# Cross-attention keys and queries transposed by VectorE in 32x32 blocks, scores on eight TensorE tiles

## The chip, the cores and the metric

The kernel runs on one core of one Trainium2 chip. A core has TensorE (matrix products and its weight loads, PE and PEld in the profile), VectorE (DVE), ScalarE (ACT), GpSimd (POOL) and SyncE (SP, which issues the DMAs). The metric is the device time of the whole program in microseconds. Before the change the median of 3 runs is 1757.12 us (1754.75 to 1758.47).

## The reference

One decoder block on x of 32 sequences of 64 tokens, 512 wide: self-attention, cross-attention on a context of the same size, and a feed-forward part, each added to x.

```python
q = (hidden_states @ Wq.T).reshape(bsz, q_len, H, HD).transpose(0, 2, 1, 3)      # H = 32 heads, HD = 128
k = (cross_attention_states @ Wk.T).reshape(bsz, kv_len, KVH, HD).transpose(0, 2, 1, 3)   # KVH = 8
v = (cross_attention_states @ Wv.T).reshape(bsz, kv_len, KVH, HD).transpose(0, 2, 1, 3)
q = _rmsnorm(q, q_norm_w)
k = _rmsnorm(jnp.repeat(k, GROUPS, axis=1), k_norm_w)       # GROUPS = 4 query heads per key head
scores = jnp.einsum('bhqd,bhkd->bhqk', q, k) * scale
probs = jax.nn.softmax(scores + attention_mask, axis=-1)
out = jnp.einsum('bhqk,bhkd->bhqd', probs, v)               # then @ Wo.T
```

The change lies between the normed q and k and the masked scores of this cross-attention.

## The kernel before

The tokens are worked in two halves of 1024, 8 tiles of 128 tokens each (a tile is two sequences). A half goes through self-attention, then cross-attention, then the feed-forward part. Cross-attention runs over the 8 key heads (groups); in each group over 4 chunks of two token tiles. That makes 32 chunks per half. The first three are prepared in `self_attention`, seven turns of a loop (`Fori`) with 4 slots each follow (`cross_attention`), and the last group is written out in `last_turn_and_ffn`, interleaved with the feed-forward part's first steps.

Every engine has its own list of instructions, written out by hand in `slot` and its neighbours; no scheduler changes it. Engines wait for each other by semaphores alone. Slot k of TensorE is a software pipeline over four chunks: `scores2` of chunk k+1, `transpose_probs` of chunk k, `transpose_chunk` of chunk k+2, `values2` of chunk k, `project_chunk_kv` and `project_chunk_q` of chunk k+3, and `outputs` of chunk k (the output projection of its two tiles). Projections are three fp32r products each (L397 to L399, high and low parts); scores, values and transposes are fp32.

- `transpose_chunk` (L646 to L655) transposes the two key tiles (L649, into a bank of acc), the four heads of the queries of one tile (L654, into y) and of the other (L415, into acc). ScalarE takes them out in `transposed_chunk` (L1040, L1043, L1047) into kt and q2t; the product of the two norm weights is applied at L1040, one number per partition.
- `scores2` contracts all 128 of the head's width: a product of 64 queries by 64 keys on 128 rows, two heads on the two column tiles (L670), all 16 into the one bank sc.
- VectorE adds the mask (L1212, `add_and_max`), takes the row maximum (L1218), later the sums (L1223), and scales keys (L1317) and queries (L1320) by their norm factors in `scale_chunk`. GpSimd computes these factors (L1617), subtracts the maximum (L1626) and normalises (L1632). ScalarE takes the exponential (L852) and the transposed probabilities (L856).
- The values' result ot goes out in a high part (ScalarE, L1053) and a low part (VectorE, `outputs_lo`, shown as w_lo<-ot at L1176), which the output projection waits for.
- PSUM has eight banks: two of acc, sc, pt (transposed probabilities), two of ot, two of y.
- Weights come as pieces through three staging buffers, high part by ScalarE (L844), low part by GpSimd (L1613), or by VectorE for two pieces at the end of slot 0.

## Time and profile before

| what | value |
|---|---|
| median of 3 runs | 1757.12 us |
| profiled execution, its own time | 1758.76 us |
| span from its first to its last instruction | 1757.0 us |
| TensorE busy | 1681.7 us, 96% |
| VectorE busy | 940.7 us, 54% |
| ScalarE busy | 742.2 us, 42% |
| GpSimd busy | 656.5 us, 37% |
| share of the chain that ended last | PE 84%, DVE 8%, POOL 3%, ACT 2%, issue 2% |

Busy is the time in which an engine runs an instruction of the program. The chain is followed back from the last instruction, at each step to what released it. Matmuls are pipelined: the time from one start to the next is what counts, and one instruction lasts longer than that.

### The profile page before, as it was taken

To read this page: it belongs to the slowest core of one execution; us is meant where nothing else is said; L and a number is where in the kernel's file an instruction comes from. 1 tells how busy PE (TensorE), PEld (TensorE's weight loads), DVE (VectorE), ACT (ScalarE), POOL (GpSimd) and SP (SyncE) were. 2 spreads that over 40 slices of the span, in tenths; PEclk is the share of its full clock that TensorE was granted. 3 is DMA by queue.
4 is the path that set the end of the run, shared out by engine and by line. 5 is a ranking of instruction groups with operands and counts; after the bars stand their busy time and mean duration, and the time that the engine had idled before them with its cause. 6 is when DMAs were issued, how large, how long until landed. Compare 5 with 4: busy or idle time off the path is not lost.

```text
span 1757.0 us, 29641 instructions
## 1 busy us (share of the span) xinstructions
PE 1681.7 (96%) x11352; PEld 1382.2 (79%) x11352; DVE 940.7 (54%) x1657; ACT 742.2 (42%) x1332; POOL 656.5 (37%) x511
## 2 busy tenths in 40 slices
PE   5999899999999999989988999999999999999898
PEld 5556788888888888778875567888888888887797
DVE  4488454454544454664545874554454545447543
ACT  2575445354444443421225744444443444434221
POOL 3595323233232332550125944232332332326400
PEclk9999999999999999999999999999999999999999
DMA  4110011011010110211121101010120201202000
GB/s 168 55 43 1 7 55 60 0 60 39 20 60 0 60 57 9 72 49 37 50 65 55 31 1 43 19 60 0 60 60 0 60 19 41 66 0 85 6 19 24
DMA packets 25871, 70.92 MB, mean 40 GB/s; under 512 B 3152, under 2 KB 3152, under 8 KB 25808
## 3 DMA queue, kind: packets, MB, share of 16 engines
q1 hardware_dynamic: 25808, 70.05, 12.8%
q8 instruction: 43, 0.70, 0.2%
q14 instruction: 20, 0.16, 0.0%
HBM read 65.85 MB, written 4.19 MB: 40 GB/s over the span
## 4 chain that ended last, share of the span: by engine, by line
PE 84%; DVE 8%; POOL 3%; ACT 2%; issue 2%; DMA 1%; POOLq 0%; SPq 0%; DVEq 0%; ACTq 0%
PE acc L397 14%; PE acc L398 13%; PE acc L399 13%; PE y L397 9%; PE y L398 9%; PE y L399 9%; PE ot L684 4%; PE sc L670 3%; PE pt L438 3%; PE acc L415 2%; PE sc L578 2%; PE y L654 1%; DVE w_lo L1176 1%; DVE pmax L1218 1%; POOL prob L1626 1%
## 5 line engine op out<-in xcount | busy, mean ns | idle before, releaser
L1626 POOL TENSOR_TENSOR prob<-prob,pmax 128x512 f32<-128x512 f32 x128 | 134.0, 1047 | 309.0 <-DVE pmax L1218 308.5
L1304 DVE TENSOR_REDUCE qkss<-kbd 128x4 f32<-128x512 f32 x128 | 87.8, 686 | 291.0 <-ACT kbd L876 291.0
L1617 POOL TENSOR_TENSOR qkrs<-qkve,mhalf 128x10 f32<-128x10 f32 x64 | 125.1, 1954 | 303.4 <-DVE qkve L1310 303.4
L397 PE MATMUL y<-w_hi 128*128 128x512 f32 x576 | 232.5, 404 | 0.9 <-DVE w_lo L1176 0.9
L397 PE MATMUL acc<-w_hi,xn_hi 128*128 128x512 f32 (+1 forms) x576 | 221.0, 384 | 11.2 <-DVE xn_lo L1176 11.2
L398 PE MATMUL y<-w_lo,w_hi 128*128 128x512 f32 x576 | 225.8, 392 | 0.0
L399 PE MATMUL y<-w_hi,w_lo 128*128 128x512 f32 x576 | 225.6, 392 | 0.0
L398 PE MATMUL acc<-w_lo,xn_hi 128*128 128x512 f32 (+1 forms) x576 | 220.2, 382 | 0.0
L399 PE MATMUL acc<-w_hi,xn_lo 128*128 128x512 f32 (+1 forms) x576 | 219.2, 381 | 0.0
L1613 POOL TENSOR_TENSOR w_lo<-stage,w_hi 128x1024 fp32r<-128x1024 f32 (+1 forms) x88 | 170.3, 1953 | 99.4 <-ACT w_hi L844 99.4
L1632 POOL TENSOR_TENSOR prob<-prob,prec 128x512 f32<-128x512 f32 x128 | 148.5, 1160 | 130.7 <-DVE prec L1226 130.7
L856 ACT COPY probt<-pt 128x512 f32<-128x512 f32 x128 | 74.2, 580 | 286.0 <-PE pt L438 286.0
L397 PE MATMUL acc<-w_hi,cx_hi 128*128 128x256 f32 x512 | 150.9, 295 | 1.7 <-DVE xn_lo L1176 1.7
L1176 DVE TENSOR_TENSOR w_lo<-ot,w_hi 128x1024 fp32r<-128x1024 f32 (+1 forms) x80 | 89.3, 1116 | 112.7 <-ACT w_hi L1053 112.4
L875 ACT COPY qb<-acc 128x512 f32<-128x512 f32 x128 | 75.1, 587 | 168.5 <-PE acc L399 168.5
L398 PE MATMUL acc<-w_lo,cx_hi 128*128 128x256 f32 x512 | 144.4, 282 | 0.0
L399 PE MATMUL acc<-w_hi,cx_lo 128*128 128x256 f32 x512 | 144.2, 282 | 0.0
L844 ACT CAST w_hi<-stage 128x1024 fp32r<-128x1024 f32 (+1 forms) x116 | 104.3, 917 | 89.3 <-DMA stage<-in_w_cross 76.7
L397 PEld LDWEIGHTS acc<-w_hi,xn_hi 128*128 128x128 f32 x576 | 110.8, 192 | 30.9 <-DVE xn_lo L1176 7.9
L397 PEld LDWEIGHTS y<-w_hi 128*128 128x128 f32 x576 | 109.0, 189 | 31.8 <-issue 11.4
L399 PEld LDWEIGHTS y<-w_hi,w_lo 128*128 128x128 f32 x576 | 109.1, 189 | 23.2
L399 PEld LDWEIGHTS acc<-w_hi,xn_lo 128*128 128x128 f32 x576 | 110.6, 192 | 20.5
(132 smaller groups left out, 3670.7 us busy)
## 6 DMA issues: line engine op xcount, KB each, us to landing
stage<-in_w_cross SPq DMA_DIRECT2D x64, 512.0 KB, 3.7
stage<-in_w_cross SPq DMA_DIRECT2D x32, 256.0 KB, 2.8
stage<-in_w_ffn SPq DMA_DIRECT2D x16, 512.0 KB, 3.5
x<-in_x SPq DMA_DIRECT2D x8, 512.0 KB, 3.7
stage<-in_w_self SPq DMA_DIRECT2D x8, 512.0 KB, 4.5
kt<-in_ctx SPq DMA_DIRECT2D x16, 256.0 KB, 2.9
out_x<-x SPq DMA_DIRECT2D x16, 256.0 KB, 2.0
stage<-in_w_self SPq DMA_DIRECT2D x4, 256.0 KB, 3.4
```

What stands on the lines that cost most here:

```text
L397: nc.tensor.matmul(target, l_hi, r_hi, start=first, stop=False)
L398: nc.tensor.matmul(target, l_hi, r_lo, start=False, stop=False)
L399: return nc.tensor.matmul(target, l_lo, r_hi, start=False, stop=last)
L844: nc.scalar.copy(target, stage[:, place.slot(n), 0:width]).then_inc(w_hi_done, 1)
L856: nc.scalar.copy(probt[:, buffer, :], pt[:]).then_inc(pt_done.sem, 1)
L875: nc.scalar.copy(qraw[:, 2 * (k % 2) + t], blocks(acc[n % 2]))
L1176: return nc.vector.tensor_tensor(target, whole, high.bitcast(F32), ALU.subtract)
L1304: nc.vector.tensor_reduce(qkss[:, k % 2, t * REP:(t + 1) * REP], qsq[:, t], AX_X, ALU.add).then_inc(q_sum.sem, 1)
L1613: nc.gpsimd.tensor_tensor(low, stage[:, place.slot(n), 0:width], high.bitcast(F32), ALU.subtract).then_inc(w_lo_done, 1)
L1617: return nc.gpsimd.tensor_tensor(target, source, mhalf[:, 0:width], ALU.pow)
L1626: nc.gpsimd.tensor_tensor(pr, pr, spread(pmax[:, buffer, :], 8, SEQ), ALU.subtract).then_inc(s_sub.sem, 1)
L1632: nc.gpsimd.tensor_tensor(pr, pr, spread(prec[:, buffer, :], 8, SEQ), ALU.mult).then_inc(s_nrm.sem, 1)
```

## The change

Keys and queries are no longer transposed by TensorE. VectorE transposes them in 32x32 blocks (`transposed`): a block stays on its 32 partitions, so that partitions 32i to 32i+31 hold block i of 32 tokens with the head's width in four pieces of 32 (j) side by side. A product then contracts 32 rows, and four of them (j = 0 to 3) are added up in PSUM. The 32 queries of block i meet the 64 keys of their sequence, its own 32 and those of the sibling block; ScalarE copies the sibling's keys to the partitions of block i (`sibling_keys`, four copies). The scores of block i go to bank i, since the four row tiles write at the same time; sc, pt and the two banks of ot become one tile, quad, of four banks. The two column tiles hold two pairs of heads. The mask is laid out anew and added in two pieces (`masked_scores`). The norm weights now lie along the free side (wrow) and are applied in `scale_chunk`, two instructions for the keys. The transposed probabilities use y[0] in place of pt. On TensorE the values move behind the projection of keys and values; ScalarE and VectorE have their lists reordered, and ScalarE and GpSimd take output weights 4 first in slot 0.

```diff
@@ TensorE
-            def transpose_chunk(place, k):
...
-                for t in range(2):
-                    ins = nc.tensor.transpose(to[:, t * P:(t + 1) * P], kv[:, 2 * (k % CHUNKS) + t, 0:P], ident[:])
...
-                for h in range(REP):
-                    ins = nc.tensor.transpose(y[0][:, h * P:(h + 1) * P], qraw[:, 2 * (k % 2), h], ident[:])
...
-                transpose_tile(*use(place, k, C_QT), qraw[:, 2 * (k % 2) + 1].rearrange("p h d -> p (h d)"))
             def scores2(place, k):
                 at = place.at
                 pe.wait_ge(qt_done.sem, at(qt_done, k + 1))
-                evacuated(pe, *use(place, k, C_QT))
+                pe.wait_ge(sib_done.sem, at(sib_done, k + 1))
                 pe.wait_ge(s_add.sem, at(s_add, k))
+                pe.wait_ge(ot_lo_done.sem, at(ot_lo_done, max(k - 1, 0)))
                 for t in range(2):
-                    for j in range(2):
-                        for b in range(2):
...
+                    for j in range(4):
+                        for i in range(4):
+                            rows = slice(32 * i, 32 * (i + 1))
+                            first = 32 * (1 - i % 2)
                             for h in range(2):
+                                ins = nc.tensor.matmul(
+                                    quad[h * SEQ:(h + 1) * SEQ, i, t * SEQ:(t + 1) * SEQ],
+                                    q2t[rows, t, j, 2 * h:2 * h + 2, :].rearrange("p h q -> p (h q)"),
+                                    k2t[rows, t, j, first:first + SEQ], start=j == 0, stop=j == 3)
@@ slot
                 scores2(place, k + 1)
-                transpose_probs(place.at, k, k % PRING)
-                transpose_chunk(place, k + 2)
-                values2(place, k)
+                transpose_probs2(place.at, k)
                 project_chunk_kv(place, k + 3)
+                values2(place, k, k + 2)
                 project_chunk_q(place, k + 3)
@@ ScalarE
-                transposed_chunk(place, k + 2)
...
+            def sibling_keys(at, k):
+                act.wait_ge(kt_done.sem, at(kt_done, k + 1))
+                for i in range(4):
+                    o = i ^ 1
+                    first = 64 * (1 - i % 2)
+                    ins = nc.scalar.copy(k2t[32 * i:32 * (i + 1), :, :, first:first + 32],
+                                         k2t[32 * o:32 * (o + 1), :, :, 32:64])
+                ins.then_inc(sib_done.sem, 1)
@@ VectorE
+            def masked_scores(at, k):
+                dve.wait_ge(sc_rdy.sem, at(sc_rdy, k + 1))
+                for t in range(2):
...
+                ins.then_inc(s_add.sem, 1)
+            def transposed(place, k):
+                at = place.at
+                dve.wait_ge(qk_nrm.sem, at(qk_nrm, k + 1))
+                dve.wait_ge(sc_rdy.sem, at(sc_rdy, k))
+                c = k % CHUNKS
+                nc.vector.transpose(k2t[:, :, :, 32:64],
+                                    kv[:, 2 * c:2 * c + 2, 0:P].rearrange("p t (j d) -> p t j d", j=4)
+                                    ).then_inc(kt_done.sem, 1)
+                for t in range(2):
+                    ins = nc.vector.transpose(q2t[:, t],
+                                              qraw[:, 2 * (k % 2) + t].rearrange("p h (j d) -> p j h d", j=4))
+                ins.then_inc(qt_done.sem, 1)
@@ slot
-                add_and_max(at, k + 1, (k + 1) % PRING)
-                outputs_lo(at, k)
+                masked_scores(at, k + 1)
+                row_max(at, k + 1, (k + 1) % PRING)
+                transposed(place, k + 2)
                 sums(at, k + 1, (k + 1) % PRING)
                 key_squares(place, k + 3)
+                outputs_lo(at, k)
```

TensorE's list at the head of the loop, before; qb holds the queries, kt the keys, a row ends with the semaphores that it waits for:

```order
L670 MATMUL sc<-kt,qb 64x64 [waits s_add]
L670 MATMUL sc<-kt,qb 64x64 x15
L436 REGISTER_ALU [waits s_nrm]
L438 MATMUL pt<-ident,prob 128x128 [waits pt_done]
L438 MATMUL pt<-ident,prob 128x128 x3
...
L649 MATMUL acc<-ident,kv 128x128 [waits acc_free1]
...
L654 MATMUL y<-ident,qb 128x128 [waits y_free]
...
L415 MATMUL acc<-ident,qb 128x128 [waits acc_free0]
...
L684 MATMUL ot<-probt,kv 128x256 [waits ot_lo_done]
```

and after, with the lines of the changed kernel:

```order
L656 REGISTER_ALU [waits sib_done,qt_done]
L658 REGISTER_ALU [waits s_add]
L667 MATMUL quad<-kt,qb 64x64 [waits ot_lo_done]
L667 MATMUL quad<-kt,qb 64x64 x63
L677 ISA [waits s_nrm]
L679 MATMUL y<-ident,prob 128x128 [waits y_free]
L679 MATMUL y<-ident,prob 128x128 x3
...
L407 MATMUL acc<-w_hi,cx_hi 128x256 [waits acc_free1]
...
L695 MATMUL quad<-probt,kv 128x256 [waits ot_lo_done,s_add]
```

Ten transposes are gone, the scores are 64 products in place of 16, and the values stand behind the 24 products that project keys and values.

VectorE's list in the last turn, behind the loop, before:

```order
L1212 TENSOR_TENSOR prob<-sc,mask 128x512
L1218 TENSOR_REDUCE pmax<-prob 128x8
L1235 TENSOR_TENSOR x<-y,x 128x512
L1196 TENSOR_SCALAR xn<-x,mv,rstd 128x512
L1176 TENSOR_TENSOR w_lo<-ot,w_hi 128x2x8x64
```

and after:

```order
L1222 TENSOR_TENSOR prob<-quad,mask 128x256 x2
L1243 TENSOR_REDUCE pmax<-prob 128x8
L1233 STREAM_TRANSPOSE kt<-kv 128x8x32
L1237 STREAM_TRANSPOSE qb<-qb 128x512 x2
L1260 TENSOR_TENSOR x<-y,x 128x512
L1204 TENSOR_SCALAR xn<-x,mv,rstd 128x512
L1184 TENSOR_TENSOR w_lo<-quad,w_hi 128x2x8x64
```

The three transposes of chunk 3 of the group stand ahead of the first layer norm of the feed-forward part.

## Rows read from the trace of the kernel before

**Rows 1.** The page: busy shares, and the last chain by engine.

```profile
PE 1681.7 (96%) x11352; PEld 1382.2 (79%) x11352; DVE 940.7 (54%) x1657; ACT 742.2 (42%) x1332; POOL 656.5 (37%) x511
...
PE 84%; DVE 8%; POOL 3%; ACT 2%; issue 2%; DMA 1%; POOLq 0%; SPq 0%; DVEq 0%; ACTq 0%
```

**Rows 2.** A stretch of the loop: length; busy us of PE, PEld, DVE, ACT, POOL; clock.

```profile
400.00:500.00 100.00, 100.00 (x728) 84.49 (x727) 49.53 (x77) 42.98 (x75) 31.56 (x22) 1.00 0.09 26
```

**Rows 3.** The last chain in order of time: start us, length us.

```profile
456.79 1.08 PE sc L670 x32
...
474.58 1.08 PE sc L670 x32
```

**Rows 4.** Timeline of TensorE in one slot: start us, length us.

```profile
474.51 1.15 PE L670 MATMUL sc<-kt,qb 128*64 128x64 f32 x32
475.59 0.66 PE L438 MATMUL pt<-ident,prob 128*128 128x128 f32 x4
476.08 0.38 PE L649 MATMUL acc<-ident,kv 128*128 128x128 f32 x2
476.30 0.60 PE L654 MATMUL y<-ident,qb 128*128 128x128 f32 x4
...
477.27 1.13 PE L684 MATMUL ot<-probt,kv 64*128 64x256 f32 x8
478.33 0.39 PE L397 MATMUL acc<-w_hi,cx_hi 128*128 128x256 f32 x1
...
481.30 0.40 PE L397 MATMUL acc<-w_hi,xn_hi 128*128 128x512 f32 x1
...
486.76 0.39 PE L397 MATMUL y<-w_hi 128*128 128x512 f32 x1
```

**Rows 5.** Products under way in 134.92 to 134.96 and in 477.26 to 477.31.

```profile
L593 PE MATMUL ot<-probt,vbd x4: 297/297/297, 134.9 to 134.9; 128*32 128x128 f32 x4
```

```profile
L684 PE MATMUL ot<-probt,kv x2: 480/480/480, 477.3 to 477.3; 64*128 64x256 f32 x2
```

**Rows 6.** VectorE: one slot's sum, groups of one slot, and the mask of slot 1.

```profile
474.40:492.20 17.80, 17.80 (x127) 15.01 (x126) 8.23 (x14) 6.51 (x12) 4.05 (x3) 1.00 0.00 0
```

```profile
L1176 DVE TENSOR_TENSOR w_lo<-ot,w_hi 128x1024 fp32r<-128x1024 f32 x1 | 1.2, 1224 | 2.5 <-ACT w_hi L1053 2.5
...
L1317 DVE TENSOR_TENSOR kv<-kv,qkrs 128x256 f32<-128x256 f32 x1 | 0.4, 426 | 0.7 <-POOL qkrs L1617 0.7
```

```profile
443.25 0.68 DVE L1212 TENSOR_TENSOR prob<-sc,mask 128x512 f32<-128x512 f32 x1
```

**Rows 7.** ScalarE: groups of one slot, and a small copy.

```profile
L1053 ACT CAST w_hi<-ot 128x1024 fp32r<-128x1024 f32 x1 | 1.0, 1017 | 0.3 <-PE ot L684 0.3
...
L1047 ACT COPY qb<-acc 128x512 f32<-128x512 f32 x1 | 0.6, 609 | 0.0
...
L1040 ACT ACTIVATE kt<-acc,qkn 128x256 f32<-128x256 f32 x1 | 0.5, 481 | 0.0
```

```profile
L972 ACT COPY vbd<-kv x64: 230/242/245, 60.1 to 1019.8; 64x64 f32<-64x64 f32 x64
```

**Rows 8.** The loop's entry: TensorE's timeline.

```profile
207.63 0.43 PE L649 MATMUL acc<-ident,kv 128*128 128x128 f32 x2 [3.78 <-DVE qb L1320]
...
211.44 0.47 PE L397 MATMUL acc<-w_hi,cx_hi 128*128 128x256 f32 x1
```

**Rows 9.** The last turn: TensorE's wait, VectorE and GpSimd at 722.

```profile
729.88 0.66 PE L415 MATMUL acc<-ident,xn 128*128 128x128 f32 x4 [2.27 <-DVE xn L1196]
```

```profile
722.27 2.40 POOL L1613 TENSOR_TENSOR w_lo<-stage,w_hi 128x1024 fp32r<-128x1024 f32 x1
...
722.34 2.62 DVE L1317 TENSOR_TENSOR kv<-kv,qkrs 128x256 f32<-128x256 f32 x1 [0.74 <-POOL qkrs L1617]
```

**Rows 10.** The page: instruction loads, and a load's time to landing.

```profile
q8 instruction: 43, 0.70, 0.2%
...
stage<-in_w_cross SPq DMA_DIRECT2D x64, 512.0 KB, 3.7
```

More of the change, by code:

```diff
@@ L221, in decoder_block @@
         qk_ve, qk_rs, qk_nrm = (count(n, 0, 0, CHUNKS, 0) for n in ("qk_ve", "qk_rs", "qk_nrm"))
-        qt_rdy, qt_done = (count(n, 0, 0, CHUNKS, 0) for n in ("qt_rdy", "qt_done"))
+        kt_done, sib_done, qt_done = (count(n, 0, 0, CHUNKS, 0) for n in ("kt_done", "sib_done", "qt_done"))
         kbd_done = count("kbd_done", 0, NSEQ, 0, 0)
@@ L306, in load_constants @@
             def load_constants():
-                sp.dma_start(qkn[:, 0:1], qn_in).then_inc(const_ld.sem, 16)
-                sp.dma_start(qkn[:, 1:2], kn_in).then_inc(const_ld.sem, 16)
-                sp.dma_start(mask[0:SEQ, :], mask_in).then_inc(const_ld.sem, 16)
-                sp.dma_start(mask[SEQ:P, :], mask_in).then_inc(const_ld.sem, 16)
+                sp.dma_start(qrow, qn_in.rearrange("d o -> o d").to_broadcast([P, HD2])).then_inc(const_ld.sem, 16)
+                sp.dma_start(wrow[:], kn_in.rearrange("d o -> o d").to_broadcast([P, HD2])
+                             ).then_inc(const_ld.sem, 16)
+                for h in range(REP):
+                    for l in range(2):
+                        sp.dma_start(mask[32 * h:32 * (h + 1), l, :], mask_in[32 * l:32 * (l + 1), :]
+                                     ).then_inc(const_ld.sem, 16)
                 sp.dma_start(f1g_raw, f1g_in).then_inc(const_ld.sem, 16)
@@ L635, in self_attention @@
                 project_chunk_q(first, 1)
-                transpose_chunk(first, 0)
                 project_out(at, NT - 1, NT)
@@ L683, in values2, with outputs @@
                         rows = slice(b * SEQ, (b + 1) * SEQ)
+                        probs = probt[rows, k % 2, t * 256:(t + 1) * 256].rearrange("p (l h q) -> p h l q", l=2, h=REP)
                         ins = nc.tensor.matmul(ot[:, b, t * 256:(t + 1) * 256],
-                                               kv[rows, 2 * (k % CHUNKS) + t, P:2 * P],
-                                               probt[rows, k % 2, t * 256:(t + 1) * 256], start=True, stop=True)
+                                               kv[rows, 2 * (k % CHUNKS) + t, P:2 * P], probs, start=True, stop=True)
                 ins.then_inc(ot_rdy.sem, 1)
-            def outputs(place, k, t, queries):
+            def outputs(place, k, t):
                 if t == 0 and k % CHUNKS == 0:
                     pieces_split(place, 5)
-                if t == 0:
-                    pe.wait_ge(qt_done.sem, place.at(qt_done, queries))
                 project_out(place.at, 2 * k + t, k + 1)
@@ L855, in evacuate_probs @@
                 act.wait_ge(pt_rdy.sem, at(pt_rdy, u + 1))
[L856 removed]
+                nc.scalar.copy(probt[:, buffer, :], pt).then_inc(pt_done.sem, 1)
             def output_hi(i):
@@ L874, in queries @@
                 act.wait_ge(q_sum.sem, place.at(q_sum, 2 * k + t - 1))
+                if k >= 2:
+                    act.wait_ge(qt_done.sem, place.at(qt_done, k - 1))
                 nc.scalar.copy(qraw[:, 2 * (k % 2) + t], blocks(acc[n % 2]))
@@ L1126, in last_turn_and_ffn @@
                 split_piece(place, 5)
-                evacuate_probs(turn.at, 3, 1)
+                evacuate_probs2(turn.at, 3)
                 rectify(0, 0)
@@ L1315, in scale_chunk @@
                 c = k % CHUNKS
-                keys = kv[:, 2 * c:2 * c + 2, 0:P]
-                nc.vector.tensor_tensor(keys, keys, spread(qkrs[:, k % 2, 2 * REP:], 2, HD2), ALU.mult)
+                for t in range(2):
+                    keys = kv[:, 2 * c + t, 0:P]
+                    nc.vector.scalar_tensor_tensor(keys, keys, qkrs[:, k % 2, 2 * REP + t:2 * REP + t + 1], wrow[:],
+                                                   ALU.mult, ALU.mult)
                 t = 2 * (k % 2)
@@ L1386, in self_attention @@
                 scale_chunk(first.at, 0)
+                transposed(first, 0)
                 key_squares(first, 1)
@@ L1390, in self_attention @@
                 variance(first.at, 1)
+                updated(7)
                 scale_chunk(first.at, 1)
-                updated(7)
                 key_squares(first, 2)
-                add_and_max(first.at, 0, 0)
+                masked_scores(first.at, 0)
+                transposed(first, 1)
+                row_max(first.at, 0, 0)
                 second_norm(7)
+                query_squares(first, 2, 0)
                 sums(first.at, 0, 0)
-                query_squares(first, 2, 0)
                 query_squares(first, 2, 1)
@@ L1501, in result @@
                                                    ALU.mult, ALU.add).then_inc(x_out.sem, 1)
-                add_and_max(turn.at, 1, 1)
-                outputs_lo(turn.at, 0)
+                masked_scores(turn.at, 1)
+                row_max(turn.at, 1, 1)
+                transposed(turn, 2)
                 sums(turn.at, 1, 1)
                 key_squares(turn, 3)
+                outputs_lo(turn.at, 0)
                 query_squares(turn, 3, 0)
@@ L1512, in last_turn_and_ffn @@
                 final_statistics(0)
-                add_and_max(turn.at, 2, 2)
+                masked_scores(turn.at, 2)
+                row_max(turn.at, 2, 2)
+                transposed(turn, 3)
                 updated(1)
@@ L1524, in last_turn_and_ffn @@
                 norm(2)
-                add_and_max(turn.at, 3, 3)
+                masked_scores(turn.at, 3)
+                row_max(turn.at, 3, 3)
                 norm_lo(1)
```

152 lines of the change are left out of this document (69 added, 83 removed).

## The prediction, made before the changed kernel ran

> **What bounds the kernel now.** I read the busy shares first, then the chain that ended last, then the chain in order of time, and last single slots of the timeline. TensorE is busy for 96% of the span and holds 84% of the last chain; no other engine is over 54% [rows 1]. The reader is to see in the busy times of a stretch that in 400 to 500 us TensorE is busy for every one of the 100 us at clock 1.00, while VectorE has half of its time free [rows 2]. The chain in order of time then shows the loop as a clock: scores (L670) come at 456.79 and again at 474.58, 17.79 us apart, and so slot after slot through both loops [rows 3]. Inside a loop slot nothing but TensorE's own list sets the time. Only at two places per half is it otherwise: at the loop's entry, where TensorE sits idle for 3.78 us [rows 8], and in the last turn, where VectorE is waited for [rows 9]. The kernel has 2 halves of 32 chunks: 28 loop slots, and 4 chunks in the last turn.
>
> One slot of TensorE [rows 4]: scores from 474.51, transposed probabilities from 475.59, transposed keys from 476.08, transposed queries from 476.30, values from 477.27, keys and values projected from 478.33, queries from 481.30, the output projection from 486.76.
>
> **TensorE's part.** The change takes the ten transposes of a chunk away (2 for keys, 8 for queries). They fill 476.08 to 477.27 [rows 4], 1.19 us for ten and the change of tile shape before the values. The four transposes of the probabilities take 0.49, so some 0.11 each after the first; ten cost 1.09 and 0.1 stays as the change of shape, which the new order has as well, between the projection of keys and values and the values. So **-1.09 us per chunk**.
>
> The scores grow from 16 to 64 products in the program, and each runs as two in the trace: 32 now (x32), 128 then. The 32 take 1.08 us: two column tiles run side by side, so that is 16 steps of 64 columns, 67 ns each with the fill. The new ones have the same 64 columns each, on 8 tiles (four of rows by two of columns): 128 / 8 is again 16 steps. What decides is whether eight tiles really overlap. The trace shows it for four and for two: of the values in self-attention four products on four column tiles begin inside a stretch of 40 ns, each 297 ns long, and the two row tiles of the values in cross-attention begin inside 50 ns [rows 5]. So the bound from below is 1.08 (no loss; a gain is excluded, since the steps are as many and as wide). The bound from above is the mean of today's 32 products, 34 ns each: 128 x 34 = 4.3 us. I take the value near the lower one, 1.12: the tiles begin well under 10 ns apart (four in 40 ns, less than their first lasts), and six more of them at some 7 ns lengthen the fill by 0.04. **+0.04 per chunk.**
>
> The Trainium skill (TensorE: Matmul & The Clock Gate, Part 3) has matmuls on different tiles start about 4 ns apart; by that the added fill is 0.02 and the sum would be 1 us better. The same page (Part 1) has start to start never below some 25 ns however small the matmul. If that held between tiles too, 128 x 25 = 3.2 us would stand in place of 1.08, and the kernel would be slower by some 65 us. Rows 5 speak against it: four begin in 40 ns. It is a case of the first rival below, between its ends.
>
> Then 17.79 becomes 17.79 - 1.09 + 0.04 = 16.74 us per slot. The slot that holds chunk 2 of a half I count with the entry, so 27 slots per half: 54 x 1.05 = **-56.7 us**.
>
> **Does another engine hold a slot of 16.7 us?** VectorE gets a transpose of the keys (128x256) and two of the queries (128x512 each), the mask in two pieces, the key scale in two. No row shows a 32x32 transpose. The nearest are two-operand or reducing operations of the same size: 0.43 for 128x256 (L1317), 0.68 for 128x512 (L1212) [rows 6]. I take 0.4 + 2 x 0.7 = 1.8; four times as slow would be 7.2. The mask adds 0.15, the keys 0.15. VectorE's 8.2 us of a slot [rows 6] become 10.3 of 16.7. The wait that could reach TensorE: the output projection needs w_lo of ot (L1176, outputs_lo), and the values now stand behind the projection of keys and values, so only the queries' 5.46 us cover it. Counted from the slot's start, the new order gives: scores to 1.1, probabilities to 1.6, keys and values to 4.5, values to 5.6, queries to 11.1. VectorE: mask 1.3 to 2.2, maximum to 2.9, transposes to 4.7, sums to about 5.6, and L1176 of 1.22 as soon as ScalarE's 1.02 (L1053) is done: 5.9 + 1.0, then to 8.2. It is due at 11.1, so 2.9 us of cover. Transposes up to 4.7 us long cost nothing in a common slot; beyond that the rest shows. ScalarE loses 0.48 + 0.61 + 0.6 = 1.7 us (L1040, L1047, and L1043 of the same shape) and gets four copies of 32 partitions by 256, between 0.24 (L972, 64 elements) and 0.48 (L1040, 256) each [rows 7]: I take 0.4, so 1.6, no change. They are wanted a slot later (scores of k+2), 8 us of cover. In slot 0 ScalarE and GpSimd now split output weights 4 first, which frees its staging buffer for the next load earlier: nothing lost. The tightest new wait is in slot 1: the values wait for the mask of the next chunk (they share its banks), and VectorE only comes to it after two weight pieces. Before, the mask starts at 443.25, 4.3 us after that slot's start at 438.93 (two of 17.79 before 474.51), and takes 0.68 [rows 6]. The new values are due 4.5 after the start, mask in two pieces done near 4.3 by the new sum, 5.1 at worst. I cost it at 0, at worst 0.6 x 14 = 8 us.
>
> **Entry.** At 207.63 TensorE has sat idle for 3.78 us until VectorE's L1320 scaled the queries of chunk 2, since their transposes come before the values of chunk 0 [rows 8]; the keys and values of chunk 3 start at 211.44. In the new order the transposes of chunk 2 are VectorE's and are wanted a slot later; TensorE projects chunk 3 as soon as the probabilities are transposed. New late ones: this normalisation, and then the mask of chunk 1, behind the scale of chunk 2. My sum: probabilities at 201, projection to 204.5, values at about 205.8 behind the mask, queries at 207; before, queries start at 214.4 (211.44 + 2.97). That is 7.4 us, of which 3.3 are three chunks' transposes; I take 6.5, and 3.3 to 8 as ends. **-13 us** for both halves.
>
> **Last turn.** Here VectorE is late: TensorE waits 2.27 us for xn (L1196), and the layer norm stands behind L1317 at 722.34, 2.62 us long beside a GpSimd split of 2.40 [rows 9]. VectorE's list also gets the transposes of chunks 2 and 3 there. The transposes of chunk 3 (1.8) and the mask (0.15) come ahead of that xn, against 1.1 us that the chain gains by starting earlier; so the norm comes about 1 us later and nothing of the four chunks' gain is kept. **+2 us** for both halves, -4 to +8 as ends.
>
> **Sum.** -56.7 - 13 + 2 = -67.7 us. The profiled execution took 1758.76 (span 1757.0, 1.76 around it); the same program after it would take 1691.1. The median of the runs shown is 1757.12, so I predict **1689.4 us**, own range 1680 to 1702.
>
> **Rivals.**
> 1. *The array takes products by their count* (slower). Mechanism: the 128 products are handed over one by one, and tiles don't help beyond what today's 32 show. For it: no row has more than 8 products in flight on tiles, and the scores today are 34 ns per product. Against: rows 5, where products begin faster than that. Price: 3.24 us more per chunk less 1.05 x 64 and the entry: 64 x 3.2 - 68 = +137, so about 1894 us. It decides from 67.7 / 64 / 96 = 11 ns for each of the 96 added products; between 0 and 11 ns it only eats the gain.
> 2. *The loop's instructions no longer stay near TensorE.* A slot has 126 products today (24 + 24 + 24, 32, 4, 10, 8) and 212 then, and as many weight loads. The profile's page has 43 packets, 0.70 MB, of instruction loads on queue q8 [rows 10], for 11352 products and 11352 weight loads that ran [rows 1]: 31 bytes for each. The loops' slots are 56 x 126 = 7056 of the products, so it looks as if a body were fetched once and kept for seven turns. If the longer one were not kept, each of the 14 turns back would wait for a fetch, 0 to 3.7 us (the landings of rows 10), partly hidden behind the queued projections: 14 x 2 = 28 us lost, 1717 us. The Trainium skill (Runtime: NRT & Kernel Launch, Instruction fetch mechanics) gives TensorE room for 2048 instructions in blocks of 256, and a taken branch to a block that is gone stalls. By its figures the body grows from about 1070 to 1740 instructions, still inside; with a block or two fetched ahead it is not. No row here can tell.
> 3. *VectorE becomes late* (transposes at half speed or held by GpSimd's splits, as L1317 was): a microsecond per slot 0 and 1 and a few in the last turn, some 20 us, 1710 us.
> 4. *The gain is more*: the entry gives 8 and the last turn nothing is lost: 1678 us.
>
> That the change doesn't do what it says I count with the first.
>
> **Chances.** Forecast 0.62; rival 1 in full 0.10, in part and still faster 0.05, in part and slower 0.04; rival 2 0.09; rival 3 0.06; rival 4 0.04. Range for 8 in 10: 1678 to 1738, which holds the forecast, rivals 2 and 3 and part of the first. A run of this kernel can tell 0.2%, 3.5 us. Faster 0.84, same 0.02, slower 0.14.
>
> **What would show it.** The slot in the chain of time at 16.7 us; the scores' x128 in 1.1 to 1.2 us (rival 1: 2 us and more); no TensorE row on transposes of keys or queries; VectorE transposes near 0.4 and 0.7 us; TensorE idle at the loop's entry under 3 us; no idle time of TensorE at the first scores of each turn (rival 2 puts it there), q8's bytes near 0.9 MB (608 more products in the program, most run as two) and not far above. Wrong is the prediction if the scores take over 1.6 us or slots of one turn differ by over 1 us.

## The result, and the profile after

The changed kernel takes 1784.68 us (median of 4 runs, 1782.13 to 1786.9), the kernel before 1756.02 beside it (4 runs). The ratio is 1.0149, 95% interval 1.0128 to 1.0171: slower by 1.5%, where 1689.4 us and a gain of 3.8% were forecast. The measured time lies outside the range of 1678 to 1738. The profiled execution has a span of 1785.2 us, 28.2 more than before.

The page of the kernel after answers to [rows 1] and [rows 10]: TensorE's busy share fell from 96% to 93%, "issue" (TensorE waits for nothing that the profile shows) grew from 2% to 4% of the last chain, and the instruction loads went from 43 packets and 0.70 MB to 162 and 2.65 MB.

```profile
PE 1667.2 (93%) x16856; PEld 1364.3 (76%) x16856; DVE 1065.0 (60%) x1977; ACT 764.7 (43%) x1396; POOL 656.0 (37%) x511
...
q8 instruction: 162, 2.65, 0.6%
...
PE 82%; DVE 8%; issue 4%; POOL 3%; ACT 2%; DMA 1%; POOLq 0%; SPq 0%; DVEq 0%; ACTq 0%
```

A slot in the timeline of TensorE after, start and length in us, answers to [rows 4]:

```profile
459.89 1.59 PE L667 MATMUL quad<-kt,qb 32*64 32x64 f32 x128
461.42 0.65 PE L679 MATMUL y<-ident,prob 128*128 128x128 f32 x4
...
464.87 1.13 PE L695 MATMUL quad<-probt,kv 64*128 64x256 f32 x8
465.93 0.50 PE L407 MATMUL acc<-w_hi,xn_hi 128*128 128x512 f32 x1
...
477.07 1.14 PE L667 MATMUL quad<-kt,qb 32*64 32x64 f32 x86
```

From scores to scores it is 477.07 - 459.89 = 17.18 us, 0.61 less than before and 0.44 more than forecast. The scores last from 459.89 to 461.42, 1.53 us, not 1.12. Nothing waits inside the slot. But four such slots are 68.72 us, and a turn is longer. The values of successive slots, first half (after 464.87 above), then second half, show where:

```profile
482.05 1.13 PE L695 MATMUL quad<-probt,kv 64*128 64x256 f32 x8
...
503.00 1.14 PE L695 MATMUL quad<-probt,kv 64*128 64x256 f32 x8
...
1211.16 1.13 PE L695 MATMUL quad<-probt,kv 64*128 64x256 f32 x8
...
1234.86 1.14 PE L695 MATMUL quad<-probt,kv 64*128 64x256 f32 x8
```

464.87 to 482.05 is 17.18; across the turn (482.05 to 503.00, 1211.16 to 1234.86) it is 20.95 in the first half and 23.70 in the second. The same view at the two places, with the idle time before a row and its releaser in brackets:

```profile
494.25 0.38 PE L667 MATMUL quad<-kt,qb 32*64 32x64 f32 x17
496.99 2.03 PE L667 MATMUL quad<-kt,qb 32*64 32x64 f32 x111 [2.35 <-issue]
...
1223.37 0.32 PE L667 MATMUL quad<-kt,qb 32*64 32x64 f32 x2
1225.69 1.57 PE L667 MATMUL quad<-kt,qb 32*64 32x64 f32 x126 [2.00 <-issue]
...
1229.55 0.80 PE L679 MATMUL y<-ident,prob 128*128 128x128 f32 x3 [1.92 <-issue]
```

The first scores of a turn break off after 17 products (2 in the second half) and TensorE sits without instructions for 2.0 to 2.6 us; in the second half a second stall of 0.9 to 2.0 us follows behind the burst. The waits of the whole trace sum these up (total us, times, longest). A loop of seven turns has six branches back, twelve in all; two of the 14 waits are under 0.3 us, and one of the 7 is at a loop's entry:

```profile
PE quad L667 <- issue: 27.4, 14, 2.6
...
PE y L679 <- issue: 10.0, 7, 2.0
PE quad L695 <- DVE prob L1222: 5.8, 2, 3.3
```

At each branch back TensorE's own sequencer shows the same: the branch (COMPARE_BRANCH; duration in ns, shortest, median and longest, with the two that leave the loop among the 14) takes 3.3 to 3.9 us where it took 0.21. First the kernel before, then after:

```profile
L708 PEldq COMPARE_BRANCH  x14: 76/208/236, 274.8 to 1572.7; - x14
```

```profile
L714 PEldq COMPARE_BRANCH  x14: 83/3486/3876, 273.4 to 1595.4; - x14
```

The products that are already queued cover this wait (the branch of 490.20 is over at 493.67, and TensorE works on without a gap up to the scores at 494.25); what shows is the next one, after the 17 products. In the one turn from 490 to 562 the instruction queue fetches nine packets:

```profile
q8 instruction: 9, 0.15, 0.9%
```

In the kernel before it fetches none from 273 to 703.

The six turns from the second to the seventh, from scores to scores (PE busy, granted clock), show the rest of the loss: 14.1 and 23.3 us idle, and a mean clock of 0.99 and 0.95.

```profile
277.46:709.98 432.52, 418.46 (x5089) 0.99 0.13 39
1147.56:1599.43 451.87, 428.56 (x5090) 0.95 0.12 37
```

The rows around the second of the turns shown above say where the clock falls (length; busy us of PE, PEld, DVE, ACT, POOL; clock):

```profile
1223.00:1228.00 5.00, 2.63 (x131) 1.88 (x131) 2.29 (x4) 1.04 (x1) 2.35 (x1) 0.93 0.03 7
1228.00:1232.00 4.00, 2.45 (x12) 2.45 (x12) 2.29 (x5) 1.62 (x3) 1.05 (x2) 0.50 0.23 66
1232.00:1236.00 4.00, 4.00 (x26) 3.49 (x24) 0.95 (x3) 1.32 (x3) 3.37 (x2) 0.73 0.12 22
```

After 5 us in which TensorE was busy for 2.63 the clock stands at 0.50 (1.2 of 2.4 GHz) for 4 us and at a mean of 0.73 in the next 4. Twenty-four slots of 17.18 are 412.3 us, so the loops lose 20.2 and 39.5 us: beyond the idle time 6.1 in the first half, where the clock falls behind three of the six stalls, and 16.2 in the second.

### The profile page after: what moved, and what is told of

The parts are those of the page before. It is cut to its first block, busy times and chain, and to the rows that moved or that the text cites. A ratio compares the mean times of both kernels' runs of the same rounds, so it can differ in the third digit from the quotient of the medians.

```text
span 1785.2 us, 40962 instructions
## 1 busy us (share of the span) xinstructions
PE 1667.2 (93%) x16856; PEld 1364.3 (76%) x16856; DVE 1065.0 (60%) x1977; ACT 764.7 (43%) x1396; POOL 656.0 (37%) x511
## 3 DMA queue, kind: packets, MB, share of 16 engines
q8 instruction: 162, 2.65, 0.6%
## 4 chain that ended last, share of the span: by engine, by line
PE 82%; DVE 8%; issue 4%; POOL 3%; ACT 2%; DMA 1%; POOLq 0%; SPq 0%; DVEq 0%; ACTq 0%
PE acc L407 14%; PE acc L408 13%; PE acc L409 13%; PE y L407 9%; PE y L408 8%; PE y L409 8%; PE quad L667 5%; PE quad L695 4%; PE y L679 2%; PE quad L588 2%; DVE w_lo L1184 1%; DVE xn_lo L1184 1%; DVE pmax L1243 1%; POOL prob L1663 1%; PE quad L448 1%
## 5 line engine op out<-in xcount | busy, mean ns | idle before, releaser
L407 PE MATMUL acc<-w_hi,xn_hi 128*128 128x512 f32 (+1 forms) x576 | 229.0, 398 | 10.5 <-DVE xn_lo L1184 10.5
L1055 ACT COPY probt<-y 128x512 f32<-128x512 f32 x64 | 37.6, 588 | 316.7 <-PE y L679 316.7
L407 PE MATMUL acc<-w_hi,cx_hi 128*128 128x256 f32 x512 | 156.7, 306 | 2.3 <-DVE xn_lo L1184 1.7
L408 PE MATMUL acc<-w_lo,cx_hi 128*128 128x256 f32 x512 | 150.8, 295 | 0.0
L409 PE MATMUL acc<-w_hi,cx_lo 128*128 128x256 f32 x512 | 150.2, 293 | 0.0
L856 ACT ACTIVATE prob<-prob 128x512 f32<-128x512 f32 x128 | 81.0, 633 | 133.3 <-POOL prob L1663 132.3
L667 PEld LDWEIGHTS quad<-kt,qb 32*64 32x64 f32 x8192 | 96.7, 133 | 50.9 <-issue 50.6
L667 PE MATMUL quad<-kt,qb 32*64 32x64 f32 x8192 | 107.1, 235 | 27.5 <-issue 27.4
L1260 DVE TENSOR_TENSOR x<-y,x 128x512 f32<-128x512 f32 x144 | 99.0, 688 | 49.2 <-PE y L409 49.2
```

The lines of the kernel that those rows point to most:

```text
L407: nc.tensor.matmul(target, l_hi, r_hi, start=first, stop=False)
L408: nc.tensor.matmul(target, l_hi, r_lo, start=False, stop=False)
L409: return nc.tensor.matmul(target, l_lo, r_hi, start=False, stop=last)
L667: ins = nc.tensor.matmul(quad[h * SEQ:(h + 1) * SEQ, i, t * SEQ:(t + 1) * SEQ], q2t[rows, t, j, 2 * h:2 * h + 2, :].rearrange("p h q -> p ...
L856: nc.scalar.activation(prob[:, buffer, :], prob[:, buffer, :], ACT.Exp).then_inc(s_exp.sem, 1)
L1260: nc.vector.tensor_tensor(x[:, i % NT, :], y[i % 2][:], x[:, i % NT, :], ALU.add).then_inc(y_free.sem, 1)
```

## The experiments

Two theories of the turns stood against each other. **Theory F**: the loop's longer body is fetched anew in every turn, rival 2 of the prediction. **Theory A**: the array itself is what is dear, rival 1. For the 0.44 us in each slot, theory I (instructions reach the array too slowly in a burst) was set against A. Ratios are to the kernel before, on the same chip. An execution and its span differ by some 2 us.

### m1_merge: half as many score products

```diff
-                            for h in range(2):
-                                ins = nc.tensor.matmul(
-                                    quad[h * SEQ:(h + 1) * SEQ, i, t * SEQ:(t + 1) * SEQ],
-                                    q2t[rows, t, j, 2 * h:2 * h + 2, :].rearrange("p h q -> p (h q)"),
+                            ins = nc.tensor.matmul(
+                                quad[:, i, t * SEQ:(t + 1) * SEQ],
+                                q2t[rows, t, j].rearrange("p h q -> p (h q)"),
```

> The changed kernel with each pair of column tiles of the scores made one product of 128 queries: 32 products in the program per chunk in place of 64, same results. The loop's turn goes from 1753 executed TensorE instructions to 1241. Theory F (fetch: the longer loop body is fetched anew in every turn, which costs 3.4 us per turn in the first half and 6.6 in the second, 70 us in all): the idle at issue at each turn is gone, q8 falls from 2.65 MB to under 1 MB, 1785 - 70 = 1715 us or less. Theory A (array: what is dear is four small accumulating products in place of one, by array time): the scores keep 1.53 us and the turns their stalls, 1785. Theory I (issue: the scores take 1.53 and not 1.12 us because TensorE is fed 256 instructions, about 8 ns each): with half of them the scores take about 1.1 us, the slot is 16.75, another 54 x 0.43 = 23 us go; F and I together 1692 us.

Measured: 1750.38 us, ratio 0.9954 (0.9939 to 0.9969). The page has few instruction loads, and TensorE's timeline shows longer scores:

```profile
q8 instruction: 46, 0.75, 0.2%
```

```profile
434.76 2.01 PE L666 MATMUL quad<-kt,qb 32*128 32x64 f32 x64
436.70 0.66 PE L678 MATMUL y<-ident,prob 128*128 128x128 f32 x4
```

Theory F holds: with the shorter body the loads are back at 0.75 MB and the idle at issue in the loop is gone (a branch back takes 0.21 us again). The forecast of the slot failed on both theories' terms: 64 products take 1.94 us (434.76 to 436.70), more than 128 narrow ones. A step of four products of 128 columns on four row tiles takes 1.94 / 16 = 0.12 us, nearly twice the step of 64 columns before (1.08 / 16 = 0.067), so I take the array as the limit here; no run separates it from another cause. The next scores start at 452.37, a slot of 17.61.

### h1_hint: the branch back announced

```diff
-                with pe.Fori(0, NG - 1) as turn:
+                with nc.Fori(0, NG - 1, engines=[mybir.EngineType.PE], hint_back_edge=True) as turn:
```

> The changed kernel with one instruction at the head of TensorE's loop that announces the branch back, so that its target may be fetched ahead; nothing else. Theory F as a cost of the turn back: the stall of 2.3 us at the first scores of each turn goes, 14 x 2.3 = 32 us, with the low clock behind it up to 14 x 3.4 = 48 us: 1737 to 1753 us, while the second stall of the second half's turns (2.0 us) stays; q8 stays at about 2.65 MB. If the stall is not at the branch but wherever 256 instructions run in 1.5 us while one block takes 0.9 to 1.4 us to come, it stays: 1780 to 1785. Theory A: nothing, 1785.

Measured: 1725.08 us, ratio 0.9803 (0.9770 to 0.9837). One instruction per turn takes back 59.6 us (1784.68 - 1725.08), more than the 32 to 48 expected.

```profile
q8 instruction: 54, 0.88, 0.2%
```

```profile
L714 PEldq COMPARE_BRANCH  x14: 80/220/258, 271.5 to 1533.9; - x14
```

```profile
275.57:687.89 412.32, 412.32 (x5089) 1.00 0.13 39
1125.67:1537.99 412.32, 412.32 (x5089) 1.00 0.13 39
```

In both loops TensorE is busy for every microsecond at clock 1.00; the same six turns took 432.52 and 451.87 us. So the fetch cost (432.52 + 451.87 - 2 x 412.32) / 12 = 5.0 us per turn back, with the low clock: 3.4 in the first half, 6.6 in the second. I had expected q8 to stay at 2.65 MB; it fell to 0.88, and from 273 to 683 not one packet is fetched. So the announcement does not only fetch the target ahead, the body now stays. Why it does is not shown by a run: fetching straight on past the loop's end, which the announcement may stop, could be what pushes a block out.

### u1_unroll: no branch on TensorE

```diff
-                with pe.Fori(0, NG - 1) as turn:
+                for turn in range(NG - 1):
```

> The changed kernel with TensorE's seven turns written out (no branch back on TensorE; the other engines keep their loops), the same products in the same order. Theory F: with no branch each block can be fetched while the one before runs; if the turn back is what costs, turns are 4 x 17.18 = 68.7 us and the time 1785 - 70 = 1715 us; if the scores' burst (256 instructions in 1.5 us) outruns the fetch by itself, stalls of 1 to 2 us appear at the scores of every slot or some, 1740 to 1800 us. q8 rises to 2.65 MB or more. Theory A: 1785.

Measured: 1726.56 us, ratio 0.9827 (0.9790 to 0.9864), the time of h1_hint.

```profile
q8 instruction: 135, 2.21, 0.5%
```

The same six turns are 412.32 us, all of them busy at clock 1.00, in either half. Here 2.21 MB are fetched, not far from the 2.65 of the changed kernel, and in the loops it costs nothing: fetched in a straight line, even the bursts of 256 never run dry. The loss lies in the taken branch to instructions that are gone, not in the amount fetched. In the first half's six turns 41 packets are fetched, some 7 a turn, where the changed kernel fetches 9: it loads about two more than the body fills, which would fit the parts at its two ends and one fetched past them. The time of 1715 us was not reached since it counted all seven turns and took 70 us for 60.

### p1_pad and p2_pad_hint: the kernel before with a longer body

```diff
+            def pad():
+                for _ in range(68):
+                    pe.wait_ge(const_ld.sem, 16 * 9)
...
                 transpose_chunk(place, k + 2)
+                pad()
                 values2(place, k)
```

and four more calls of `pad` in the slot (two waits become one instruction); p2_pad_hint announces the branch besides.

> The kernel before, with 170 waits that are always satisfied added to each of the loop's slots on TensorE, spread between the projections: 680 instructions more per turn, as long a loop body as the changed kernel's, without its scores or its bursts. Theory F: the body is fetched anew in every turn (q8 from 0.70 to 2 to 3 MB) and the turn back stalls by about 2.3 us: 14 x 2.3 = 32 us or, with the low clock behind a stall, 48: 1789 to 1805 us; nothing by Theory A: 1757, with the waits themselves hidden behind products in the queue (if they are not, every slot is longer by the same amount).

> p1_pad (the kernel before with 680 more instructions per turn) with the announced branch. p1_pad took 2196 us, most of it in the added waits themselves (about 100 us of each turn in place of 71), so only the difference between these two tells of the fetch. Theory F: q8 falls from 2.57 MB to under 1 MB, the turns fall by 2 to 7 us each, 30 to 100 us in all, and the turns of both halves, 101 and 106 us in p1_pad, become equal. If the refetch is particular to the scores' bursts: no difference, 2190 to 2200 us.

Measured: 2195.75 us without (4 runs) and 2114.45 with the announcement (2 runs). The waits were dear themselves: with both kernels TensorE sits idle at issue in every slot of the loop, so p1_pad alone says little of the time; it missed its expectation by some 400 us. The pair does say something: 81 us between them, q8 at 157 packets (2.57 MB) against 49 (0.80 MB), a branch back of 3.3 to 3.8 us against 0.22, and at the first scores of a turn a stall of over 4 us only in p1_pad, as here at 1487.46:

```profile
L717 PEldq COMPARE_BRANCH  x14: 76/3516/3841, 304.9 to 2012.8; - x14
```

```profile
1487.46 1.74 PE L670 MATMUL sc<-kt,qb 128*64 128x64 f32 x32 [4.58 <-issue]
```

The refetch therefore needs no scores on eight tiles and no VectorE transposes. This body has the changed kernel's length, and that is enough.

### b1_hint: the announcement alone

> The kernel before with the announced branch alone. Its body of 1073 executed instructions stays near TensorE, so by Theory F there is nothing to gain: 1755 to 1759 us, turns 71.15. If the branch cost something there too, up to 14 x 0.3 us = 4 us less.

Measured: 1757.34 us, ratio 0.9998 (0.9987 to 1.0009), 43 packets as before. Where the body stays anyway, the announcement is worth nothing.

### c3_three: a body between the two

```diff
-                    for j in range(4):
+                    for j in range(3):
```

and `stop=j == 2`, without the announcement. It leaves a quarter of each score's sum out.

> The changed kernel, without the announced branch, with one of the four accumulated products of each score left out: 1497 executed TensorE instructions per turn, between m1_merge's 1241 (kept) and the changed kernel's 1753 (fetched anew in every turn). Theory F says that there is a size from which it decides, not a slope: q8 is either under 1 MB with turns of 4 slots exactly, or 2.3 MB and more with a stall of about 2 us per turn. I expect the first: about 1785 - 61 (fetch) - 56 x 0.34 (a third of the way is 0.34 us per slot) = 1705 us. The scores by count: 0.15 + 31 products at 9 ns + 65 at 11.5 = about 1.18 us.

Measured: 1712.49 us in a single run.

```profile
q8 instruction: 50, 0.82, 0.2%
```

```profile
462.98 1.25 PE L667 MATMUL quad<-kt,qb 32*64 32x64 f32 x96
464.17 0.66 PE L679 MATMUL y<-ident,prob 128*128 128x128 f32 x4
```

The body with 180 products per slot stays (its branch back takes 0.21 us, and no packet is fetched from 273 to 678); the one with 212 doesn't. That is what a size from which it decides would give, as expected, with one kernel on either side of it. The scores take 1.19 us for 96 products (1.18 expected).

### c1_half, c2_small and r1_order: what 128 products in a burst cost

All three are h1_hint with one edit. c1_half leaves half of each score's sum out (`stop=j == 1` goes with it):

```diff
-                    for j in range(4):
+                    for j in range(2):
```

> h1_hint with two of the four accumulated products of each score left out (64 of the head's 128 numbers are contracted): 32 program products per chunk, one burst. Theory I: 8 steps of 58 ns, the scores take 0.5 to 0.6 us, the slot 16.2 us. Theory A (12 ns each): 0.77 us, the slot 16.4. By either no slot waits at issue.

c2_small:

```diff
+                            queries, keys = (SEQ, SEQ) if j == 0 else (48, 32)
...
-                                    quad[h * SEQ:(h + 1) * SEQ, i, t * SEQ:(t + 1) * SEQ],
+                                    quad[h * SEQ:h * SEQ + queries, i, t * SEQ:t * SEQ + keys],
```

and the two operands are cut in the same way, so parts of the sums are missing.

> h1_hint with three quarters of the scores' products made smaller: for j = 1 to 3 a product takes 48 of the 64 queries (columns of the weights) and 32 of the 64 keys (columns that move); the sums are incomplete. The number of instructions stays. A step of eight products takes 58 ns where nothing else holds it, so by the array a small step should take some 45 ns and none of the 12 small steps more than now. Theory A (the array needs 10.8 ns for a product of this shape, (1.53 - 0.85 us) / 64): the scores fall from 1.53 to about 1.2 us and the slot to 16.8. Theory I (instructions reach the array at 5 to 6 ns each once the first 31 products are out, whatever their size): 1.50 to 1.55 us, slot 17.15 to 17.2.

r1_order:

```diff
-                        for i in range(4):
-                            rows = slice(32 * i, 32 * (i + 1))
-                            first = 32 * (1 - i % 2)
-                            for h in range(2):
+                        for h in range(2):
+                            for i in range(4):
+                                rows = slice(32 * i, 32 * (i + 1))
+                                first = 32 * (1 - i % 2)
```

> h1_hint with the eight products of a step in another order: the four row tiles of one column tile, then the four of the other. Same instructions. Theory I and a cost that goes by count: no change, 1725 us, scores 1.53. If two products in a row on the same 32 rows hold each other up: the scores fall towards 16 x 58 ns + 0.15 = 1.08 us, the slot to 16.75, the time to 1700. If instead neighbours on different rows hold each other up: slower than 1725.

Measured: c1_half 1686.95 us (2 runs, ratio 0.9593, 0.9572 to 0.9613), c2_small 1714.91 in a single run, r1_order 1722.73 (ratio 0.9805, 0.9788 to 0.9821). The scores and the row that follows them in c1_half, then in c2_small:

```profile
452.58 0.91 PE L667 MATMUL quad<-kt,qb 32*64 32x64 f32 x64
453.43 0.66 PE L679 MATMUL y<-ident,prob 128*128 128x128 f32 x4
```

```profile
461.42 1.48 PE L668 MATMUL quad<-kt,qb 32*64 32x64 f32 x128
462.83 0.66 PE L680 MATMUL y<-ident,prob 128*128 128x128 f32 x4
```

64 products take 0.85 us, 96 take 1.19 (c3_three), 128 take 1.53: a straight line of 10.6 ns per product. That is near A's guess of 0.77 for the half and far from I's 0.5 to 0.6. But with three quarters of the products smaller, by a quarter in the weights and by half in what moves, the scores fall only to 1.41 (461.42 to 462.83), where A wanted 1.2, and in r1_order they still last 1.53. Neither theory holds as put. What the runs say is that these small products cost by their count, hardly by their size, and that those of 128 columns (m1_merge) cost 1.94 us / 64 = 30 ns each; that this is their width is not shown. Whether the count is paid where instructions are handed over (each product brings a weight load, so 5.3 ns per instruction) or between the tiles stays open.

### s1_split and w1_quarter: two tries at shorter scores

Both start from h1_hint. s1_split issues the scores in two bursts:

```diff
             def slot(place, k):
-                scores2(place, k + 1)
+                scores2(place, k + 1, (1,))
...
                 outputs(place, k, 0)
+                scores2(place, k + 2, (0,))
                 outputs(place, k, 1)
```

> The changed kernel with the announced branch (h1_hint), and the scores of a chunk issued in two bursts of 32 program products (one token tile each): the first tile's between the two output projections of the slot before, the second at the head of the slot. Theory I (the scores take 1.53 us because TensorE runs out of prefetched instructions in a burst of 256, and gets about 8 ns each after that): a burst of 128 starts from a full queue, takes 8 steps of 58 ns, 0.47 to 0.55 us; the scores fall from 1.53 to about 1.0 us, the slot from 17.18 to 16.7, 54 x 0.5 = 27 us: 1725 - 27 = 1698. Theory A (the array itself takes 12 ns per product of this shape): the two bursts take 0.77 us each and the time is that of h1_hint, 1725. Rival on the other side: the first burst, half a slot earlier, waits for the sibling keys of ScalarE; the slot is then longer than 17.18 and the time over 1725.

Measured: 1748.81 us, ratio 0.9938 (0.9920 to 0.9956), 24 us slower than h1_hint.

```profile
465.75 0.91 PE L668 MATMUL quad<-kt,qb 32*64 32x64 f32 x64
466.59 0.50 PE L407 MATMUL y<-w_hi 128*128 128x512 f32 x1
```

The first of the two is shown; each takes 0.84 to 0.85 us as in c1_half, 1.69 together: 0.16 more than one burst. The next such row starts at 483.32, so the slot is 17.57 us, 0.39 more than 17.18; the other 0.23 lie outside the bursts, and what they are stays open. Theory I, by which a rested queue would make both short, fails here. Nothing in the loop waits; the sibling keys were in time.

w1_quarter takes one of the four accumulated products on wide tiles:

```diff
+                            width = 4 if j == 3 else 2
+                            for h in range(0, REP, width):
```

> h1_hint with the last of the four accumulated products (j = 3) taken for all four heads at once, 128 queries on a tile of 32 rows and 128 columns, the other three as before: 56 program products per chunk in place of 64, same results. From m1_merge a step of such tiles takes 111 ns, from before a step of 64 columns 58. Theory I (a burst costs 10.6 ns for each of its 128 products because of the number of instructions): 112 products in place of 128 save 16 x 10.6 = 0.17 us, as long as the array is not the limit: 12 steps of 58 and 4 of 111 are 1.14 us, less than 112 products at 10.6 (1.19): scores 1.53 to 1.36, slot 17.18 to 17.01, 56 x 0.17 = 10 us, 1724 to 1714. Theory A (the array, by the width of what is loaded): at least as long as now, 1.53 to 1.75 us, 1724 to 1736.

Measured: 1763.74 us, ratio 1.0030 (1.0017 to 1.0042), 39 us slower than h1_hint.

```profile
455.51 2.25 PE L668 MATMUL quad<-kt,qb 32*64 32x64 f32 x112
457.69 0.55 PE L680 MATMUL y<-ident,prob 128*128 128x128 f32 x3
```

2.18 us for 112 products, 0.65 more than for 128 of one width, and more than the 1.94 of 64 wide ones. I had left out the change of shape. The scores change between 64 and 128 columns three times inside this burst; at 12 steps of 0.096 (1.53 / 16, eight tiles as measured) and 4 of 0.12 the burst would be 1.6 us, so about 0.55 is left for them, some 0.2 each. That split is argued; the total is measured.

## Why the prediction was wrong, step by step

**What bounds the kernel** was right: TensorE's list sets every common slot.

**The ten transposes** were right. 17.79 - 1.09 + 0.45 (scores) is 17.15, against 17.18 measured.

**The scores** were mis-sized: +0.04 was forecast, +0.45 measured (1.53 against 1.08). I took the value near the lower bound because four products in [rows 5] begin inside 40 ns, and argued that eight would. They do at first, but over the burst each product adds 10.6 ns, to a fixed 0.17. With the 0.03 above this makes 0.44 x 54 = 24 us of the error. It lay within rival 1: (1.53 - 1.08) / 96 = 4.7 ns per added product, under the 11 from which that rival decides, so it ate gain and didn't turn the sign. The Trainium skill (TensorE: Matmul & The Clock Gate, Part 1) has about 25 ns as the least between starts; across different tiles these rows go below it, and its 4 ns between starts on different tiles (Part 3) is not reached as a mean over a long burst.

**Another engine holding the slot**: right. VectorE's transposes take 0.43 for the keys and 1.26 for the two of the queries (0.4 and 1.4 forecast), the mask 0.76, and ScalarE's four copies 1.65 (1.6):

```profile
461.52 0.76 DVE L1222 TENSOR_TENSOR prob<-quad,mask 128x256 f32<-128x256 f32 x2 [0.40 <-PE quad L667]
...
462.92 0.43 DVE L1233 STREAM_TRANSPOSE kt<-kv 128x256 f32<-128x256 f32 x1
463.27 1.26 DVE L1237 STREAM_TRANSPOSE qb<-qb 128x512 f32<-128x512 f32 x2
```

The values' new wait on the mask doesn't show in slot 1 of the turns; all of its 5.8 us in the waits are at the two entries.

**Entry**: direction right, size off. The mask of chunk 1 does stand behind the scale of chunk 2, as the text said, but VectorE gets to it later. h1_hint, whose entry is the changed kernel's, in the first half, VectorE and then TensorE:

```profile
205.83 2.70 DVE L1343 SCALAR_TENSOR_TENSOR kv<-kv,qkrs,wrow 128x128 f32<-128x128 f32 x2 [1.48 <-POOL qkrs L1654]
...
209.59 0.74 DVE L1222 TENSOR_TENSOR prob<-quad,mask 128x256 f32<-128x256 f32 x2
```

```profile
210.39 2.08 PE L695 MATMUL quad<-probt,kv 64*128 64x256 f32 x8 [3.33 <-DVE prob L1222]
212.39 0.79 PE L407 MATMUL acc<-w_hi,xn_hi 128*128 128x512 f32 x1
```

The queries start at 212.39, not at 207. The two key scales that I put at 0.58 in sum last 2.70 beside a GpSimd split. The new wait of 3.33 us took the place of the 3.78 that was removed. From the scores of chunk 1 to those of chunk 2 it is 23.38 and 23.40 us before, 22.02 and 20.61 in h1_hint. With what the transposes of chunks 0 and 1 save, and all else outside the slots, some 7.5 of the 13 us remain; that is the rest of the sum below, not a reading of its own.

**Last turn**: +2 forecast. TensorE runs out of instructions there too, in h1_hint as well:

```profile
709.54 1.14 PE L695 MATMUL quad<-probt,kv 64*128 64x256 f32 x8 [2.26 <-issue]
713.93 1.11 PE L425 MATMUL acc<-ident,xn 128*128 128x128 f32 x4 [3.25 <-DVE xn L1204]
716.01 0.76 PE L407 MATMUL y<-w_hi 128*128 128x512 f32 x1 [0.97 <-issue]
```

Against [rows 9] that is 2.26 + 0.97 of issue and 1.0 more for xn. From the first to the last scores of the last turn it is 33.99 and 32.10 us before, 36.63 and 36.56 in h1_hint: +7.1 for both halves. Since u1_unroll waits for instructions there just as long, the branch is not the reason; what is late stays open.

**The step that failed** is the one that treated the longer instruction list as free in the forecast and gave rival 2 a chance of 0.09 and 28 us. Its place (the first scores of each turn) and its mark (q8 far above 0.9 MB) came true word for word. Its price there was half of what it came to: per turn back one stall of 2.0 to 2.6 us, in the second half another of 0.9 to 2.0, and a low clock behind them, 5.0 us in all where I took 2, with 12 turns back and not 14. I had counted the body at 1740 instructions against the 2048 that the Trainium skill (Runtime: NRT & Kernel Launch, Instruction fetch mechanics) gives TensorE, and stopped at "still inside". The runs put the edge between 1497 and 1753 executed instructions of a turn, below that figure. What had to be counted was what a turn fetches, by the trace nine packets; by the figures of that section of the Trainium skill, as an estimate, 2048 instructions in blocks of 256 are eight blocks. That would be my own "with a block or two fetched ahead it is not", which I wrote and didn't work out. The same section of the Trainium skill also says that a taken branch out of a two-block window stalls and that long straight code streams; u1_unroll agrees with the second, while bodies of 1241 and 1497 instructions, more than four blocks of its 256, stayed without stalls, against the window of two.

The sum, in spans: h1_hint (1724.1) measures -32.9 from before (1757.0). Of it -32.5 are the 54 slots, where -56.7 was forecast: 24 of the error, the scores'. The last turns are +7.1 where +2 was forecast, and the rest, the entries with all else outside the slots, is -7.5 where -13 was: 5 each. The refetch adds 61.1 (1785.2 - 1724.1), and the change stands at +28.2. The refetch alone would have left the forecast a gain (-67.7 + 61.1 = -6.6), and so would the other errors alone; the kernel became slower by both together.

The best version run is the changed kernel with its branch announced: 1725.08 us in h1_hint and 1722.73 in r1_order, which are the same within their spread and 2% under the kernel before. With the branch announced the change is worth making; as it stood, the loop around it cost it the gain.

## What to carry to other kernels

When a change lengthens a loop's body on TensorE (no run here shows another engine), count the instructions of the body before and after (a product is two with its weight load), and look at the bytes of the instruction queue after: if they are many times those of the program, the body is being fetched every turn, and the duration of the loop's branch in the trace shows it too (3.5 us against 0.2). Announcing the branch, writing the turns out or shortening the body cured it here, and each is one small experiment. Price a burst of small products on many tiles by its count from a trace, not by the steps of the array, and expect each change of tile shape inside a burst to cost something (some 0.2 us here, by the estimate at w1_quarter).

## What the runs showed of the hardware that I had not expected

- A loop body that stays near TensorE costs nothing at its branch, whose 0.2 us hide behind queued products; one that doesn't costs 5.0 us per turn here, of which idle time is 37.4 / 12 = 3.1 and the rest is for the most part the granted clock at 0.50.
- The announcement lowered the loads from 162 packets to 54, and to none inside the loop: it kept the body, it didn't only hide the fetch.
- Products of 64 columns on eight tiles go at 10.6 ns each in bursts of 64, 96 and 128; merging two column tiles into one of 128 columns makes the same scores slower (1.94 us against 1.53).
- Waits that are always satisfied are not free on TensorE: (2114.45 - 1757.34) / (14 x 680) = 38 ns for each instruction of them. In the trace of p2_pad_hint they stand 106 ns apart, so products already queued covered the rest.
